# Token lists of a mixture-of-experts layer made in two parts: 51 columns, then 144

## The reference, cut to what matters

```python
x = _rmsnorm(hidden_states, ln_weight).reshape(-1, H)      # 1024 tokens, H = 512
probs = jax.nn.softmax(x @ router_weight, axis=-1)         # 16 experts
top_vals, top_idx = jax.lax.top_k(probs, 4)                # 4 experts for each token
gate, up = split(x @ gate_up_proj[e])                      # for each expert, 1024 wide
expert_out = (silu(gate) * up) @ down_proj[e]
routed = sum over a token's four experts of prob * expert_out
shared = (silu(x @ shared_gate_w) * (x @ shared_up_w)) @ shared_down_w
return routed + shared
```

## Time and profile before

| what | us |
|---|---|
| median of 3 runs | 1019.28 |
| lowest and highest run | 1013.74 and 1027.17 |
| the profiled execution | 1016.47 |
| its span (first to last instruction) | 1014.8 |
| PE busy | 934.1 (92%) |
| DVE busy | 651.1 (64%) |
| ACT busy | 538.2 (53%) |

### The profile page before, as it was taken

How to read it: one execution, slowest core, us unless ns; L and a number is a source line. 1 busy time by engine, 2 the same in 40 slices (tenths; PEclk the granted TensorE clock), 3 DMA queues, 4 the chain that set the end, 5 groups by cost and what they waited for, 6 DMA issues and landing times. The chain is left out here.

```text
span 1014.8 us, 21177 instructions
## 1 busy us (share of the span) xinstructions
PE 934.1 (92%) x7748; PEld 615.5 (61%) x7749; DVE 651.1 (64%) x1272; ACT 538.2 (53%) x857; POOL 140.2 (14%) x165
## 2 busy tenths in 40 slices
PE   5999987999999999999999999999999949976796
PEld 4545534776676666676677667667754438852453
DVE  5388694756765555765566665665667766677773
ACT  3676775456554554564556555645653122235674
POOL 0000102020111010111022012102207700002000
PEclk9999997999999999999999999999999979987998
DMA  8770738578776666766667767866886600000001
GB/s 292 258 240 2 271 130 229 204 234 265 231 246 205 194 211 216 240 236 217 194 228 264 250 200 234 262 207 224 261 256 198 168 9 0 1 0 1 1 21 63
DMA packets 164883, 181.76 MB, mean 179 GB/s; under 512 B 54610, under 2 KB 132434, under 8 KB 164851
## 3 DMA queue, kind: packets, MB, share of 16 engines
q1 hardware_dynamic: 152338, 147.35, 44.9%
q0 software_dynamic: 9808, 32.12, 9.9%
q10 hardware_dynamic: 2704, 1.87, 0.6%
HBM read 155.09 MB, written 14.68 MB: 167 GB/s over the span
## 5 line engine op out<-in xcount | busy, mean ns | idle before, releaser
L1090 DVE SCALAR_TENSOR_TENSOR w_lo<-raw_first,w_hi 128x1024 f16<-128x1024 f32 x144 | 172.5, 1222 | 77.9 <-ACT w_hi L581 77.9
L848 PE MATMUL pa<-x,w_hi 128*128 128x256 f16 (+2 forms) x576 | 171.5, 298 | 7.6 <-DVE between L1097 5.0
L849 PE MATMUL pa<-x,w_hi 128*128 128x256 f16 (+2 forms) x576 | 171.3, 297 | 0.0
L850 PE MATMUL pa<-x,w_lo 128*128 128x256 f16 (+2 forms) x576 | 171.2, 297 | 0.0
L848 PE MATMUL pb<-x,w_hi 128*128 128x256 f16 (+2 forms) x576 | 170.6, 296 | 0.0
L850 PE MATMUL pb<-x,w_lo 128*128 128x256 f16 (+2 forms) x576 | 170.6, 296 | 0.0
L849 PE MATMUL pb<-x,w_hi 128*128 128x256 f16 (+2 forms) x576 | 170.6, 296 | 0.0
L581 ACT ACTIVATE w_hi<-raw_first 128x1024 f16<-128x1024 f32 x144 | 147.7, 1049 | 2.5 <-DMA raw_first<-in_gate_up 2.5
L589 ACT CAST early<-between 128x320 f16<-128x320 f32 (+1 forms) x144 | 68.4, 475 | 148.3 <-DVE between L1097 148.3
L1090 DVE SCALAR_TENSOR_TENSOR w_lo<-raw_last,w_hi 128x1024 f16<-128x1024 f32 x72 | 88.2, 1225 | 73.2 <-ACT w_hi L581 73.2
L1102 DVE TENSOR_TENSOR early<-between,early 128x320 f16<-128x320 f32 (+1 forms) x144 | 74.0, 514 | 74.1 <-ACT early L589 74.0
(11 more groups left out here) (273 smaller groups left out, 1615.5 us busy)
## 6 DMA issues: line engine op xcount, KB each, us to landing
raw_first<-in_gate_up SPq DMA_DIRECT2D x96, 512.0 KB, 4.7
raw_last<-in_gate_up SPq DMA_DIRECT2D x32, 512.0 KB, 4.2
raw_first<-in_down SPq DMA_DIRECT2D x32, 512.0 KB, 4.5
raw_last<-in_down SPq DMA_DIRECT2D x32, 512.0 KB, 3.6
chunks<-in_f SPq DMA_DIRECT2D x16, 704.0 KB, 4.8
slot_y<-chunks POOLq DMA_DIRECT2D x16, 512.0 KB, 3.2
chunks<-in_f SPq DMA_DIRECT2D x6, 768.0 KB, 4.8
raw_first<-in_sgate SPq DMA_DIRECT2D x6, 512.0 KB, 5.6
```

Source lines behind the costliest of these rows:

```text
L848: T.matmul(out, hi_a, hi_b, start=first, stop=False, **flags)
L849: T.matmul(out, hi_a, lo_b, start=False, stop=False, **flags)
L850: return T.matmul(out, lo_a, hi_b, start=False, stop=last, **flags)
L1090: V.scalar_tensor_tensor(w_lo[:, j % RING, c], raw[j % RING][:, c], W_SCALE, w_hi[:, j % RING, c], ALU.mult, ALU.subtract).then_inc(split_ ...
```

## The change

The 195 columns are made in two parts. The first 51 (SOON_COLS, 17 units of three columns) are those of the first round and the spare unit; the other 144 serve later rounds. `mark` now writes `at_row` and 51 columns of `at_col`, in four parts, and PE waits for each part just ahead of its eight matmuls. `mark_late` writes the other 144 columns of all 32 groups, and `sum_late_lists` adds them in another PSUM bank, ahead of the last of the four steps of `down(0, SHARED, 1)`. DVE's order is another one: all marks come first, with `lo(0, 5, 0)` ahead of the last quarter; then the copy of the first lists; only then `hidden(0, 7)` and `hidden_low(0, 6)` and `(0, 7)`, `mark_late`, two `lo` of unit 1, the copy of the late lists, `add_shared` and three more `lo`. PE's second down half waits for the first half of its weight piece at its beginning and for the second half in its middle. PE and POOL wait for the late lists ahead of their loops.

```diff
--- before.py
+++ after.py
@@ -29,6 +29,7 @@
 SLOTS = MAX_ROUNDS * ROUND_SLOTS
 UNIT_COLS = -(-CAP // P)
 SLOT_COLS = (MAX_ROUNDS * EXPERTS + 1) * UNIT_COLS
+SOON_COLS = (EXPERTS + 1) * UNIT_COLS
 NARROW = 2 * P
 W1, W3 = 1408, 1408 // P
 ROUND = 12582912.0
@@ -239,7 +240,8 @@
         pt = bank("pt")
         pg = bank("pg")
         gate_ps, up_ps, y_ps = pa, pb, [ps, pt, pg, pe_]
-        list_ps = gate_ps[0][:, 0:SLOT_COLS]
+        soon_ps = gate_ps[0][:, 0:SOON_COLS]
+        late_ps = up_ps[1][:, CAP:CAP + SLOT_COLS - SOON_COLS]
         third_ps = y_ps[2][:, 0:KC * THIRD].rearrange("p (k n) -> p k n", k=KC)
 
         x_in = [sem(f"x_in{n}") for n in range(BATCH)]
@@ -289,6 +291,7 @@
         turned_in = sem("turned_in")
         listed = sem("listed")
         placed = sem("placed")
+        late_placed = sem("late_placed")
         list_summed = sem("list_summed")
         ids_ready = sem("ids_ready")
         rows_in = [sem(f"rows_in{j}") for j in range(UNIT_COLS)]
@@ -316,7 +319,7 @@
         SHARED = tiles_of(HALF)
         HALVES = [(j, part) for j in range(PIECES) for part in range(2)]
         AHEAD = 5
-        MARKS = 2
+        MARKS = 4
         MARK = NT * TOPK // MARKS
 
         def zn(t):
@@ -478,6 +481,7 @@
             pool.wait_ge(listed, 1)
             gather_rows(lists)
             n = rounds_of(pool)
+            pool.wait_ge(listed, 2)
             with pool.Fori(0, n * EXPERTS) as u:
                 gather_next(u)
                 store(u)
@@ -861,9 +865,19 @@
             def sum_lists():
 
                 pe.wait_ge(hid_ready, FH + 1)
-                pe.wait_ge(placed, MARKS)
                 for i in range(NT * TOPK):
-                    mm = T.matmul(list_ps, at_row[:, i, :], at_col[:, i, :], start=(i == 0), stop=(i == NT * TOPK - 1))
+                    if i % MARK == 0:
+                        pe.wait_ge(placed, i // MARK + 1)
+                    mm = T.matmul(soon_ps, at_row[:, i, :], at_col[:, i, 0:SOON_COLS], start=(i == 0),
+                                  stop=(i == NT * TOPK - 1))
+                mm.then_inc(list_summed, 1)
+
+            def sum_late_lists():
+
+                pe.wait_ge(late_placed, 1)
+                for i in range(NT * TOPK):
+                    mm = T.matmul(late_ps, at_row[:, i, :], at_col[:, i, SOON_COLS:SLOT_COLS], start=(i == 0),
+                                  stop=(i == NT * TOPK - 1))
                 mm.then_inc(list_summed, 1)
 
             def gate_up(U, m, g, n):
@@ -883,7 +897,7 @@
             def down(U, tiles, d, first_unit=False, last_unit=False):
                 wide = tiles[-1] < P
                 j = 4 + d
-                pe.wait_ge(split_ready, U * (2 * PIECES) + 2 * (j + 1 + RING))
+                pe.wait_ge(split_ready, U * (2 * PIECES) + 2 * (j + 1 + RING) - (1 if first_unit and d else 0))
                 if d == 0 and not first_unit:
                     pe.wait_ge(y_taken, U)
                 hi_w, lo_w = down_view(w_hi[:, j % RING, :]), down_view(w_lo[:, j % RING, :])
@@ -901,6 +915,10 @@
                     steps = [(k, i) for i in range(len(tiles)) for k in range(DOWN_K)]
                     pe.wait_ge(h_ready, U * FH + FH)
                 for k, i in steps:
+                    if first_unit and d == 1 and k == DOWN_K // 2 and i == 0:
+                        pe.wait_ge(split_ready, U * (2 * PIECES) + 2 * (j + 1 + RING))
+                    if first_unit and d == 1 and k == DOWN_K - 1 and i == 0:
+                        sum_late_lists()
                     m, w = d * DOWN_K + k, tiles[i]
                     c = slice(i * P, i * P + w)
                     if i == 0 and not (d == 1 and last_unit):
@@ -987,6 +1005,7 @@
             down(0, SHARED, 0, first_unit=True)
             sum_lists()
             down(0, SHARED, 1, first_unit=True)
+            pe.wait_ge(listed, 2)
 
             n = rounds_of(pe)
             with pe.Fori(0, n * EXPERTS) as u:
@@ -1193,9 +1212,17 @@
 
                 for i in range(part * MARK, (part + 1) * MARK):
                     V.tensor_scalar(at_row[:, i, :], place16[:, 0:P], at_f[:, 0, i:i + 1], None, ALU.is_equal)
-                    ins = V.tensor_scalar(at_col[:, i, :], place16[:, :], at_f[:, 1, i:i + 1],
-                                          token_ids[:, i // TOPK:i // TOPK + 1], ALU.is_equal, ALU.mult)
+                    ins = mark_columns(i, 0, SOON_COLS)
                 ins.then_inc(placed, 1)
+
+            def mark_columns(i, c0, c1):
+                return V.tensor_scalar(at_col[:, i, c0:c1], place16[:, c0:c1], at_f[:, 1, i:i + 1],
+                                       token_ids[:, i // TOPK:i // TOPK + 1], ALU.is_equal, ALU.mult)
+
+            def mark_late():
+                for i in range(NT * TOPK):
+                    ins = mark_columns(i, SOON_COLS, SLOT_COLS)
+                ins.then_inc(late_placed, 1)
 
             def add_shared():
 
@@ -1321,17 +1348,24 @@
             hidden(0, 6, HALF, first_unit=True)
             hidden_low(0, 5, HALF)
             mark(0)
-            hidden(0, 7, HALF, first_unit=True)
             mark(1)
-            hidden_low(0, 6, HALF)
+            mark(2)
             lo(0, 5, 0)
-            hidden_low(0, 7, HALF)
+            mark(3)
             lo(0, 5, 1)
             dve.wait_ge(list_summed, 1)
-            V.tensor_copy(lists[:, :], list_ps).then_inc(listed, 1)
-            for j, half in HALVES[0:AHEAD]:
+            V.tensor_copy(lists[:, 0:SOON_COLS], soon_ps).then_inc(listed, 1)
+            hidden(0, 7, HALF, first_unit=True)
+            hidden_low(0, 6, HALF)
+            hidden_low(0, 7, HALF)
+            mark_late()
+            for j, half in HALVES[0:2]:
                 lo(1, j, half)
+            dve.wait_ge(list_summed, 2)
+            V.tensor_copy(lists[:, SOON_COLS:SLOT_COLS], late_ps).then_inc(listed, 1)
             add_shared()
+            for j, half in HALVES[2:AHEAD]:
+                lo(1, j, half)
             n = rounds_of(dve)
             with dve.Fori(0, n * EXPERTS) as u:
                 unit(u + 1, CAP, lambda m: None)
```

## The result

The changed kernel takes 1026.66 us (median of 20 runs), the kernel before 1020.29 (20 runs): a ratio of 1.0068, 95% interval 1.0052 to 1.0083. It is slower by some 6 to 7 us where 1.7 us less were forecast, and outside the range given.

What follows compares the result with a forecast made beforehand. PE, 92% busy, bounds the kernel, so unit 1's start sets the end: 173.67 - 172.0 = 1.7 us earlier, taken from 1017.9, the middle of known times, gives 1016.2 us; range 1010 to 1022.5.

Steps and rivals of the forecast that it cites:

- The new waits of POOL and PE on the late lists hold only the next unit's gather, which isn't due until that unit's end.: Ahead of the POOL and PE loops: the added waits were taken not to delay unit 1's start.
- unit 1 at 172.0: First routed unit on PE: starts 0.4 us after the third transpose lands at 171.6, instead of at 173.67.
- I take 0.10: DVE's marks ahead of the gathers: step in us for one at_col of 51 columns, against 0.24 for 195.
- my bounds of 0.08 and 0.16: DVE's 51-column mark: steps in us of rows with 16 and 128 columns, taken as lower and upper limit.
- 6 us or more to land: Sign to look for: unit 1's transposes, issued near 161.7 behind SP's weight loads, take this long.
- the loads come too late, and it gets slower: Rival: marks at 0.16 and slow transposes start unit 1 1.6 us later than before; 1019.5 us, chance 0.15.
- The half-clock start: Unit 1's first matmuls at clock 0.50: 3.2 us long, costing 1.6 us before, left unchanged.
- The loop: Expert loop, 213 to 830 us: whatever moves the first unit's start moves the end by the same amount.

Runs made afterwards that it cites:

- e1: Changed kernel with PE's wait for the late lists moved from ahead of the loop into both branches: 1023.88 us, ratio 1.0038.
- e2: Kernel before with one more PE wait, for unit 1's transposes, ahead of the loop: 1026.22 us, ratio 1.0077.
- e3: Changed kernel with hidden(0, 7) back ahead of the list copy, PE's wait still ahead of the loop: 1022.01 us, ratio 1.0025.
- e4: Changed kernel with PE's wait inside both branches and hidden(0, 7) back ahead of the list copy: 1020.24 us, ratio 1.0007.
- e10: Changed kernel with PE's wait inside the branches and, on ACT, make_ternary(8) ahead of hidden_high(0, 7): 1021.64 us, ratio 1.0005.
- e6: Changed kernel with hidden(0, 7) back ahead of the list copy, PE's wait inside the branches, and the branch bodies swapped: 1018.12 us, ratio 0.9979.

## Why the prediction was wrong

*The step that failed* is this one: "The new waits of POOL and PE on the late lists hold only the next unit's gather, which isn't due until that unit's end." I priced PE's wait by its condition and not by what its sequencer has to do behind it. The row for it was in the trace before: the branch at L994, 4.0 us from 169.1. It ended 0.2 us ahead of the transposes, so it was no one's releaser and stood in no list of waits. The same wait moved behind the branch takes 5.2 us off the start of unit 1 (e1), and a wait put into the kernel before at that place makes it slower by a ratio of 1.0077 (e2). The forecast had unit 1 at 172.0, 32.6 us behind the start of the first down half; it came at 42.8, 10.2 later, and by e1's trace about half of that is this step.

*A term mis-sized.* "I take 0.10" for a mark of 51 columns; it is 0.21, outside my bounds of 0.08 and 0.16. The bounds came from rows with one operation and at most one scalar operand per partition, while `at_col` has two of each; the two sizes that were then run, 51 and 144, show a price that is nearly all fixed (0.21 and 0.23). Which of the two differences makes the price wasn't tried. The lists were there 14.2 us behind the first mark instead of 10.8, and what is put behind them came 7.7 us later instead of 4.3.

*Right in kind.* The transposes queue behind the loads, as forecast ("6 us or more to land": the first took 8.7). With the true price of the marks, the rival "the loads come too late, and it gets slower" is what happened up to the transposes: that rival put them 1.6 us later, they came 2.4 later. It got a chance of 0.15. Its condition held, since the third transpose landed later than before; but the start was set later still, by the branch, which neither the forecast nor any rival had.

*Two floors, not one sum.* The code load and the transposes are two floors side by side, not two terms: e1 takes away one and stops at the other, e3 the other way round. Only with both moved is the loss gone, as far as the intervals tell (e4 and e10).

*The half-clock start*, left as it was in the sum, took 5.0 us at 0.50 instead of 3.2, which costs 0.9 us more. Its length doesn't follow the idle time ahead of it: 3.2 us after 6.33 idle in e1, 5.7 after 4.11 in e4. What sets it stays open.

*The loop* passed the start on whole, as forecast. Unit 1 starts 8.5 us later than before, counted from the first down half, and the last unit, behind the loop, 9.4 later; the 0.9 more is the half-clock start. The first matmul of the last unit, before and changed:

```profile
751.58 0.38 PE L848 MATMUL pa<-x,w_hi 128*128 128x512 f16 x1
762.56 0.38 PE L852 MATMUL pa<-x,w_hi 128*128 128x512 f16 x1
```

The medians differ by 6.4 all the same. The two traces are single executions of kernels whose runs spread over 9 to 13 us, and from the last unit to the end, where the change has no part, they differ by 1.9 the other way (263.2 us before, 261.3 changed).

## What to carry to other kernels

A wait ahead of a loop or a branch is priced by the code behind it too: put it inside the body, as late as it can stand, and look in the view of the branch's line for the visit that takes microseconds. Before an instruction is moved behind a copy, follow all that stands in order behind its successor, down to the DMA queue and the chunk that a load waits for. This short instruction was not made cheap by fewer columns: take such a price from a row with the same operations and operands.

## What the runs showed that I had not expected

- The first taken jump over a body of PE's loop took 3.9 to 6.6 us in all twelve kernels, and ended 1.4 to 1.5 us after a block of 16 KB of q8. Every later branch on that line took 0.09 to 0.24, in the swapped kernels even the first jump over the other body (e6: 0.24 at 215.4). Swapping the bodies moves the long jump to the end of the first unit and doesn't remove it. Why it comes only once, no run shows.
- A transpose issued behind loads of 2 MB keeps SP itself: the first held it 4.9 us in the changed kernel (from 167.07; the next one starts at 172.09), against a step of 1.3, so that the loads behind it go late as well.
- One f16 `at_col` instruction costs 0.21, 0.23 and 0.24 us for 51, 144 and 195 columns.
